# Order of the row-maximum steps and the score groups on TensorE in a cross-attention kernel

## The reference

```
q   = layernorm(x) @ Wq * 64 ** -0.5          # 256 x 1024
k,v = split(media @ Wkv)                      # 1601 x 1024 each
sim = where(mask, q k^T, -big)                # for each head 256 x 1601
out = softmax(sim) @ v
x   = x + tanh(attn_gate) * (out @ Wo)
x   = x + tanh(ff_gate) * (gelu(layernorm(x) @ W1) @ W2)
```

## Time and profile before

| | |
|---|---|
| median of 3 runs | 939.61 us (937.93 to 944.74) |
| profiled execution, its time | 945.04 us |
| its span on the core | 943.2 us |
| mean granted TensorE clock | 0.969 |
| busy: TensorE, VectorE, ScalarE, GpSimd | 860.3, 610.4, 442.6, 393.1 us |

### The profile page before, as it was taken

One profiled execution on the slowest core, in us unless ns is written; L12 is line 12 of the kernel. 1 busy time (PEld: TensorE's weight loads), 2 busy tenths in 40 slices (PEclk: granted clock), 3 DMA queues, 4 the chain that ended last, 5 costly groups with the idle time before them and its releaser, 6 DMA issues.

```text
span 943.2 us, 18307 instructions
## 1 busy us (share of the span) xinstructions
PE 860.3 (91%) x7811; PEld 720.0 (76%) x7811; DVE 610.4 (65%) x941; ACT 442.6 (47%) x663; POOL 393.1 (42%) x179
## 2 busy tenths in 40 slices
PE   3589999999999999999999999999998789967996
PEld 2488887788888878888887888888876568846884
DVE  5766798968658888775788868666865132442243
ACT  2255545655445556454554655445544231414141
POOL 0035555556635655555555556635655400000000
PEclk9689999999999999999999999999999899988999
DMA  7100001000000100000000000000024000002000
GB/s 250 33 1 2 1 1 37 1 1 2 1 1 1 36 2 2 2 1 1 2 1 1 2 1 2 1 1 1 2 60 135 1 1 1 1 23 69 0 0 22
DMA packets 19629, 16.61 MB, mean 18 GB/s; under 512 B 849, under 2 KB 18658, under 8 KB 19426
## 3 DMA queue, kind: packets, MB, share of 16 engines
q1 hardware_dynamic: 19554, 15.51, 5.4%
HBM read 14.46 MB, written 1.05 MB: 16 GB/s over the span
## 4 chain that ended last, share of the span: by engine, by line
PE 78%; DVE 11%; ACT 4%; POOL 3%; issue 2%; DMA 2%; SPq 1%; DVEq 0%; POOLq 0%; ACTq 0%
PE psum L910 20%; PE psum L924 16%; PE psum L313 14%; PE psum L881 6%; PE psum L847 4%; PE psum L947 3%; PE psum L980 3%; PE psum L989 3%; PE psum L1035 2%; POOL acc L404 2%; DVE mx L663 2%; PE psum L940 1%; DVE k_lo L656 1%; ACT v L466 1%; DMA wq<-in_L_xattn_Wq_dram 1%
## 5 line engine op out<-in xcount | busy, mean ns | idle before, releaser
L404 POOL TENSOR_TENSOR acc<-acc,ring 128x1024 f32<-128x1024 f32 x128 | 306.5, 2394 | 18.7 <-POOL acc L404 0.4
L663 DVE TENSOR_REDUCE mx<-psum 128x2 f32<-128x800 f32 (+2 forms) x256 | 245.3, 990 | 85.3 <-PE psum L881 77.8
L481 ACT ACTIVATE ring<-psum 128x1024 f32<-128x1024 f32 x192 | 197.0, 1027 | 77.3 <-PE psum L910 71.0
L399 POOL TENSOR_TENSOR acc<-ring 128x1024 f32<-128x1024 f32 x32 | 76.7, 2398 | 322.8 <-ACT ring L481 322.8
L924 PE MATMUL psum<-ring,v 128*64 128x256 f32 (+1 forms) x1664 | 186.7, 381 | 1.8
L924 PEld LDWEIGHTS psum<-ring,v 128*64 128x64 f32 (+1 forms) x1664 | 116.7, 137 | 60.6 <-DVE k_lo L656 3.9
L910 PE MATMUL psum<-nm,maskrow 64*128 64x256 f32 (+1 forms) x832 | 125.9, 298 | 2.2 <-DVE maskrow L645 1.6
L910 PE MATMUL psum<-q_hi,k_hi 64*128 64x256 f32 (+1 forms) x832 | 119.2, 282 | 0.0
L910 PE MATMUL psum<-q_lo,k_hi 64*128 64x256 f32 (+1 forms) x832 | 118.8, 281 | 0.0
L910 PE MATMUL psum<-q_hi,k_lo 64*128 64x256 f32 (+1 forms) x832 | 118.6, 280 | 0.0
L881 PE MATMUL psum<-k_hi,q_hi 64*128 64x400 f32 (+1 forms) x512 | 97.2, 378 | 12.9 <-DVE mx L663 8.3
(11 more groups left out here) (149 smaller groups left out, 1366.6 us busy)
## 6 DMA issues: line engine op xcount, KB each, us to landing
nat<-in_ctx_dram SPq DMA_DIRECT2D x8, 768.0 KB
w<-in_L_xattn_W_dram SPq DMA_DIRECT2D x2, 1024.0 KB, 7.9
xs<-in_x_dram SPq DMA_DIRECT2D x4, 256.0 KB, 5.3
ring<-in_L_xattn_Wkv_dram SPq DMA_DIRECT2D x1, 1024.0 KB, 7.2
wq<-in_L_xattn_Wq_dram SPq DMA_DIRECT2D x1, 1024.0 KB, 9.3
wo<-in_L_xattn_Wo_dram SPq DMA_DIRECT2D x1, 1024.0 KB, 10.3
out_dram<-t_res SPq DMA_DIRECT2D x4, 256.0 KB, 2.2
mask<-in_mask_BxS_bk_dram SPq DMA_DIRECT2D x4, 200.1 KB, 5.9
```

The lines of the kernel that those rows point to most:

```text
L399: nc.gpsimd.tensor_tensor(acc[:, :, :, :], ring[:, 0, :, :, :], ring[:, 1, :, :, :], ALU.add)\
L404: nc.gpsimd.tensor_tensor(acc[:, :, :, :], acc[:, :, :, :], ring[:, g, :, :, :], ALU.add)\
L481: nc.scalar.activation(ring[:, g, :, :, :], score_set[m % 2].rearrange("p (h i q) -> p h i q", h=2, i=2), ACT.Exp).then_inc(S["p_ready"], 1)
L663: nc.vector.tensor_reduce(mx[:, t, :, c], aux_pair[BANK[item] // 2][:, :, 0:min(c1, KEYS) - c0], axis=AX.X, op=ALU.max).then_inc(S["m_max" ...
```

## The change

In `row_phase`, M1 stays behind S0. Before, M1 and M2 followed each other and each further S had one M in front of it (M7 in front of S6). After, each of the first six S has one M in front of it and S6 has two, M6 and M7.

```diff
 def row_phase(j):
-    out = [("M", j + 1, 0), ("S", j, 0), ("M", j + 1, 1)]
-    for g in range(1, KEY_GROUPS):
-        out += [("M", j + 1, g + 1), ("S", j, g)]
-    return out
+    out = []
+    for g in range(KEY_GROUPS - 1):
+        out += [("M", j + 1, g), ("S", j, g)]
+    return out + [("M", j + 1, KEY_GROUPS - 1), ("M", j + 1, KEY_GROUPS), ("S", j, KEY_GROUPS - 1)]
```

## The result

The changed kernel takes 955.6 us (median of 4 runs, 954.84 to 957.16) against 939.62 (937.93 to 944.74); the ratio is 1.0137 with a 95% interval of 1.0095 to 1.018. The profiled execution took 955.62 us with a span of 953.8. The forecast was 945.6 with a range to 955, so the measured median lies 0.6 us above the range: right that a new wait costs more than the old one gave back, and too small by 10 us of 16. From profile to profile the forecast was +5.2 us and the measurement +10.6. A later set of runs gave the same ratio, 1.0137 (1.0098 to 1.0175), at 955.25 against 944.31 us.

The account below looks back on a forecast made before the run. TensorE, busy 91% of the span, was taken as the bound. Plain phases +6.2, extras of phases 3 and 4 +1.7, last batch +1.6, phase 5 -4.3 gave +5.2 us; +6 on the median made 945.6, range 936 to 955.

Parts of the forecast that it names:

- (1): Ordinary row phases on TensorE: M2's wait for M0's maximum goes, a gain of 0.25 us each.
- (3): End of row phase: the item behind S6 waits for M6's maximum, 0.53 us more idleness, net +0.28 us per ordinary phase.
- (2): ScalarE's exponentials in the row phase: two waits replace two, no net change; M6 starts 7.1 us after M0.
- (4): M7's pair of banks comes free one maximum later: a further +0.28 us in phase 3 and in phase 4.
- (5): Row phase 5: S1 fills part of M2's wait, M0 to W 9.65 us; gains 4.3 us, or 1.4 if the clock falls.
- (6): Last batch: phases 2 to 5 get longer, phase 6 gains 0.44 us through earlier GpSimd sums; together +1.6 us.
- (7): VectorE 0.24 us later behind N: pauses ahead of L cover it, cost nothing; uncovered, 7.4 us over 31 phases.
- Rival B: Short idleness in some 30 phases makes TensorE's granted clock fall, 1.4 us a fall, up to 966 us; chance 0.17.
- Rivals C: The new wait is swallowed by a ScalarE and VectorE chain in full phases, gains stand alone, 929 us; chance 0.14.
- D: Rival: exponentials pace the row phase whatever M does, nothing measurable changes, 940 us; chance 0.07.

Follow-up runs that it names:

- Experiment 8: Changed kernel with the adjacent pair (M5, M6) in front of S5 and L672's negative maxima written by a reduce: 937.37 us, ratio 0.9938 to the kernel before.
- experiment 1: Changed kernel with L672's negative maxima written by a tensor_reduce, the sign moved into the matrix R multiplies with: 944.45 us, ratio 0.9998 to the kernel before.
- experiment 2: Kernel before, old order, with L672's negative maxima written by a tensor_reduce: 939.18 us, ratio 0.9958 to the kernel before.
- experiment 5: Changed kernel again, unaltered, in the same set as other runs: 955.25 us, ratio 1.0137 to the kernel before.
- experiment 6: Changed kernel with an extra GpSimd add over 380 columns ahead of each pair's sums, L672 as it was: 950.04 us, ratio 1.0077 to the kernel before.

## Why the prediction was partly wrong, step by step

**(1) and (3), the old wait and the new one: right.** M2 has no wait; the item behind S6 starts at M6 + 1.45; +0.28 us in each ordinary row phase, 5.9 us over the 22 where I had 6.2. Experiment 8 against 1 gives the price of the pair's place in front of S6, 0.24 us a phase, by itself.

**(2), the exponentials: right.** Two pieces of 1.04 us before, two after; M6 at M0 + 7.09.

**(4), M7's pair in phases 3 and 4: right without the collision, far too small with it.** I had +0.28 in each beyond the plain one. With the reduce the full phases 3 and 4 are longer by 0.18 us each than in the old order with the reduce (experiments 1 and 2). In the changed kernel they are longer by 1.56 and 1.22.

**(5), phase 5: the sign was right, the size too small, and the step was not right.** I took M2 to stay at M0 + 3.4 and got 9.65 us from M0 to W; it was 8.54, so 7.7 us were gained in three batches where I had 4.3. VectorE's lateness itself shrank. In its queue F (the division, L693) and U (L677), which needs GpSimd's last sum, stand ahead of C, Z and M0's maximum. In batch 1 before, GpSimd's last add ends 3.88 us ahead of M0 (333.33 against 337.21), F takes 1.78 us and U starts 3.67 us ahead:

```profile
331.83 1.78 DVE L693 TENSOR_TENSOR ot<-od,rec 128x256 f32<-128x256 f32 x1
333.54 0.68 DVE L677 TENSOR_TENSOR acc<-acc 128x512 f32<-128x512 f32 x1
```

After, that add ends 5.88 us ahead of M0 (337.82 against 343.70), because S1 is earlier and phase 4 longer, F takes 0.42 us and U starts 5.03 us ahead:

```profile
338.32 0.42 DVE L693 TENSOR_TENSOR ot<-od,rec 128x256 f32<-128x256 f32 x1
338.67 0.68 DVE L677 TENSOR_TENSOR acc<-acc 128x512 f32<-128x512 f32 x1
```

M0's maximum then starts 1.04 us after M0 where it started 2.40 us after, and holds M2 no more. Without collisions of L672 (experiments 1 and 2) phases 5 gain 4.2 us. That this is my 4.3 is luck: 2.9 of the 4.3 were two falls of the clock, and neither of those profiles has one there. Over all 32 instances F's median went from 1078 to 425 ns (min/median/max in ns; before, then after): 26 of 32 were long before, 10 after, and each long one ends 0.28 us behind an add. So F, which reads two tiles in SBUF, met GpSimd's adds too; no run takes that exposure away by itself.

```profile
L693 DVE TENSOR_TENSOR ot<-od,rec x32: 424/1078/2478, 94.8 to 747.0; 128x256 f32<-128x256 f32 x32
```

```profile
L693 DVE TENSOR_TENSOR ot<-od,rec x32: 424/425/1369, 93.8 to 759.0; 128x256 f32<-128x256 f32 x32
```

**(6), the last batch: phases 2 to 5 about right, phase 6 wrong in sign.** R waits 3.00 us in place of 1.20, because L672 ahead of it takes 1.57; D behind it no longer waits. +1.8 us where I had -0.44.

```profile
728.94 0.66 PE L886 MATMUL psum<-identr,negl 128*128 128x128 f32 x2 [3.00 <-DVE negl L672]
```

**(7), "Behind the later N ... I cost it at nothing": this is the step that failed.** It is the term that I put at nothing. I counted N as late by the 0.24 us of the maxima and took its own instructions at their old lengths. Its second instruction grew by 1.37 us in ordinary phases, far beyond the 0.2 us pauses ahead of L that I had named as cover. In phases 3 and 4 the T items of VectorE stand right behind it and V4 and K1 wait for them, 1.20 and 0.79 us; in phase 8 K2 waits for L0, 0.47 us. Experiments 1 and 5 put the price of this at 10.8 us of the 955.3. The order alone costs 5.3 us (experiments 1 and 2), where my sum without falls of the clock had +8.1; the difference is the phases 5, 4.2 us gained in place of 1.4. The bound that I gave for the loss of the cover, 0.24 us in each of 31 phases, bounded the wrong quantity. What could have been seen beforehand: three of L672's 32 instances in the trace of before took 1.07 to 2.12 us where 29 took 0.23, and F took anything from 0.42 to 2.48. I had not looked at the spread of either.

**Rival B, the clock: not what happened.** The new waits of 0.2 to 1.2 us left the granted clock at full speed (1.00 from 60 to 716 us), and in phases 5, where it had fallen in two batches, it no longer did (stretch, its length, TensorE's busy time, granted clock, share of DMA, GB/s):

```profile
343.70:352.30 8.60, 8.39 (x123) 1.00 0.00 0
522.00:530.60 8.60, 8.39 (x123) 1.00 0.01 2
308.00:310.00 2.00, 1.77 (x14) 1.00 0.00 0
60.00:716.00 656.00, 634.19 (x6484) 1.00 0.02 5
727.70:734.40 6.70, 5.46 (x26) 0.50 0.05 12
```

The last row is its first fall behind the start-up, at the level of 1.2 GHz; it begins towards the end of R's wait of 3.00 us.

The rule on frequent short pauses that I cited from the Trainium skill did not bite at this size. **Rivals C and D** are refuted: the row phases are longer, and the full phases 2, 6, 7 and 9 behind them give only 0.1 us back in twelve. The mechanism that decided, a collision of VectorE with GpSimd, was in none of the rivals. The Trainium skill has it: "SBUF — State Buffer", section "Who interferes with whom", says that VectorE and GpSimd share a pair of ports, that a `tensor_scalar` on SBUF may take it, that whoever issues first holds it for its whole instruction while the other fully blocks, and that a `tensor_reduce` never contends. The runs agree for VectorE's side: 1.58 us for L672, up to just behind the end of the add, and 0.29 us for the reduce inside an add, as for each of its 32 instances in experiment 1. Two things are not as sharp as the page has them. An L672 issued 0.09 us ahead of an add's end was not held (experiment 6), and where L672 came first the add grew by at most 0.07 us (2.46 against 2.39), although it started 0.19 us ahead of L672's end.

## What to carry to other kernels

When a change moves work on one engine, ask not only who waits for whom, but which instructions of VectorE and GpSimd now overlap, and compare the spread of each instruction's duration with its median: a line with 29 instances at 0.23 us and three at 1 to 2 us is at the mercy of its place. A tuned order may rest on such a coincidence, here a gap of 0.14 us, so that any reordering looks bad, whatever it is worth in itself. First take the exposure away (here an instruction of another kind for the same values), then judge the order.

## What the runs showed of the hardware that was not expected

- A VectorE `tensor_scalar` of 128x128 from SBUF to SBUF, 0.23 us alone, took 1.58, 1.82, 1.34 and 2.27 us when issued inside a GpSimd add of 2.36 us or so. In every long instance of the traces it ended 0.08 to 0.09 us after the add.
- Issued 0.09 us ahead of an add's end (308.78 against 308.86, experiment 6) it still took 0.23 us.
- A VectorE `tensor_tensor` of 128x256 with both inputs in SBUF (F), 0.42 us alone, took up to 2.48 us beside GpSimd's adds and then ended 0.28 us after the add.
- Two adjacent M steps pay 0.15 to 0.25 us wherever they stand, as the second waits for the maximum of the step two before it: 0.63 us before in the chain, 0.61 from M6 to S6 after, 0.52 in front of S5, where two steps take 0.37 or 0.38.
- 0.39 us more of useless work on GpSimd for each pair made the changed kernel 27 us faster (950.0 against 977.3), as it moved a gap of 0.14 us onto one VectorE instruction.
